# Diagonals of two heads as units under one mask product, four row slots, rows loaded by two engines, chunk-wise experts, and a tail among the maxima

## What is computed

```python
q, k, v = (x @ Wq.T + bq), (x @ Wk.T + bk), (x @ Wv.T + bv)      # 16 heads of depth 8
scores = einsum("bqhd,bkhd->bhqk", q, k) * attn_scale[0]
scores = where((qb >= kb) & (ik - iq - 2 * (kb - qb) >= 1), -inf, scores)   # chunks of 64
x = layernorm(x + (softmax(scores) @ v) @ Wo.T + bo)
s = sigmoid(x @ gate_weight.T)          # top 4 of 8 groups, then top 6 of 32, weights scaled by 2.5
routed = sum_e combine[:, e] * ((silu(x @ gate_e.T) * (x @ up_e.T)) @ down_e.T)
x = layernorm(x + routed + shared_expert(x))
```

## Time and profile before

| what | value |
|---|---|
| median of three runs | 492.0 us |
| profiled execution: its own time, and its span | 491.96 us, 490.0 us |
| first matmul of maxima | 32.6 us |
| first matmul of exponentials | 69.3 us |
| end of the last maxima | 262.4 us |
| end of the last values | 310.0 us |
| expert loop at its regular pace | from 321.4 us |
| PE, DVE, ACT, POOL busy | 422.9, 343.7, 220.7, 131.6 us |

### The profile page before, as it was taken

One profiled execution on the slowest core, in us unless ns is written; L12 is line 12 of the kernel. 1 busy time (PEld: TensorE's weight loads), 2 busy tenths in 40 slices (PEclk: granted clock), 3 DMA queues, 4 the chain that ended last, 5 costly groups with the idle time before them and its releaser, 6 DMA issues.

```text
span 490.0 us, 7996 instructions
## 1 busy us (share of the span) xinstructions
PE 422.9 (86%) x2856; PEld 218.9 (45%) x2856; DVE 343.7 (70%) x763; ACT 220.7 (45%) x299; POOL 131.6 (27%) x232
## 2 busy tenths in 40 slices
PE   6339979998698789798899997789999999999992
PEld 2225432433233233232333452467767666666661
DVE  3826978997588758589586448167768967865763
ACT  4600026675467647467477678322235233223220
POOL 4000014826545557444335434000000000000000
PEclk9855558999689979799799999899999999999998
DMA  4352430020211202101000000143213233443330
GB/s 142 131 183 96 113 96 3 4 93 7 62 51 34 84 7 71 50 3 61 7 1 3 1 1 3 44 137 88 106 70 107 102 119 105 135 134 101 110 108 21
DMA packets 27180, 34.26 MB, mean 70 GB/s; under 512 B 5893, under 2 KB 16261, under 8 KB 27141
## 3 DMA queue, kind: packets, MB, share of 16 engines
q1 hardware_dynamic: 26512, 33.41, 21.7%
q10 hardware_dynamic: 628, 0.34, 0.3%
HBM read 29.08 MB, written 4.46 MB: 68 GB/s over the span
## 4 chain that ended last, share of the span: by engine, by line
PE 60%; DMA 10%; DVE 9%; SPq 9%; POOL 4%; issue 4%; ACT 2%; POOLq 0%; DVEq 0%; ACTq 0%
PE ps L1235 12%; PE ps L1140 10%; PE ps L1100 8%; SPq L516 7%; PE ps L1207 6%; PE ps L1209 6%; PE ps L1208 6%; DVE mx L827 6%; DMA rows_k<-scratch 5%; PE ps L1123 4%; DMA w_raw<-in_unitT 2%; PE ps L1104 2%; PE ps L1160 2%; SPq L550 1%; ACT probs L727 1%
## 5 line engine op out<-in xcount | busy, mean ns | idle before, releaser
L827 DVE TENSOR_REDUCE mx<-ps 128x1 f32<-128x512 f32 (+3 forms) x320 | 180.9, 630 | 56.3 <-PE ps L1104 53.7
L727 ACT ACTIVATE probs<-ps 128x1024 f32<-128x1024 f32 (+2 forms) x160 | 143.5, 943 | 82.9 <-PE ps L1123 82.2
L1100 PE MATMUL ps<-rows_k,rows_q 48*128 48x512 bf16 (+3 forms) x384 | 111.9, 378 | 35.2 <-DMA rows_k<-scratch 26.7
L1140 PE MATMUL ps<-probs,Vg 128*32 128x512 f32 (+3 forms) x768 | 87.0, 526 | 7.5 <-POOL probs L625 6.5
L795 ACT ACTIVATE sg<-ps 128x512 f32<-128x512 f32 x68 | 40.8, 599 | 101.5 <-PE ps L1209 100.3
L1123 PE MATMUL ps<-rows_q,rows_k 51*128 51x512 bf16 (+3 forms) x384 | 72.9, 350 | 3.8 <-issue 2.5
L1207 PE MATMUL ps<-x1hi,w_hi 128*128 128x512 f32 x136 | 74.9, 551 | 0.0
L1100 PEld LDWEIGHTS ps<-rows_k,rows_q 48*128 48x128 bf16 x384 | 31.7, 99 | 95.5 <-DVE mx L827 55.3
L1035 DVE TENSOR_TENSOR au<-ps,sg 128x512 f32<-128x512 f32 x64 | 44.1, 689 | 38.0 <-PE ps L1235 37.0
L1235 PE MATMUL ps<-hh,w_down 128*128 128x512 f32 x136 | 69.8, 595 | 0.8 <-DVE hh L1040 0.8
L621 POOL TENSOR_SCALAR_AFFINE_SELECT probs<-probs 64x512 f32<-64x512 f32 x64 | 42.6, 666 | 69.0 <-ACT probs L727 66.6
(11 more groups left out here) (106 smaller groups left out, 316.7 us busy)
## 6 DMA issues: line engine op xcount, KB each, us to landing
comb_rows<-weights SPq DMA_DIRECT2D x128, 128.0 KB, 2.9
scratch<-oT SPq DMA_DIRECT2D x8, 384.0 KB, 3.0
w_raw<-in_unitT SPq DMA_DIRECT2D x17, 128.0 KB, 2.3
rows_q<-scratch SPq DMA_DIRECT2D x16, 96.0 KB
rows_k<-scratch SPq DMA_DIRECT2D x16, 96.0 KB
w_down<-in_unitT SPq DMA_DIRECT2D x1, 1088.0 KB, 7.7
xT<-in_xT SPq DMA_DIRECT2D x4, 256.0 KB, 3.9
rows_q<-scratch SPq DMA_DIRECT2D x16, 64.0 KB
```

Source lines behind the costliest of these rows:

```text
L727: act.activation(dst, src, ACT.Exp).then_inc(exps_ready, 1)
L827: dve.tensor_reduce(m_[:, part, j:j + per, qt], src, AX.X, ALU.max).then_inc(max_read, 1)
L1100: mm = pe.matmul(bank(b, m, at), rows_q[f:f + ROWS, s, p + qt * P:p + (qt + 1) * P], rows_k[f:f + ROWS, s, p + k0:p + k0 + m], start=True, ...
L1140: mm = pe.matmul(ps[STRIP * j:STRIP * (j + 1), VALUES * BANK:VALUES * BANK + m], Vg[:, g % 2, kt, j, :], probs[:, (NB * g + b) % SLOTS, j, ...
```

## The change

- **Units of the maxima.** A diagonal of 128 columns is a part of its own, always for two heads in one bank; the mask is added by one matmul of 256 columns (`identb` times `mask_qk`, broadcast over both heads), which opens the accumulation. The other keys follow in up to two more parts. NM becomes 48. `mx` gets three parts, and one `tensor_reduce` joins them.
- **Last group.** The last group's units are ordered with the first 512 queries ahead, and its maxima are joined, transposed, split and stored in two halves (`TOPS`); half of these stores is issued by ACT.
- **Row slots and loads.** NS is 4. Group 0's `rows_k` is issued by ACT, its `rows_q` by SP; waits for stored q and k parts are apart. Biases are loaded from ACT's queue. The x and constant loads and `w_down` come after the stores of group 0's maxima and the rows of group 3.
- **Front.** All eight projections have a bank of their own; all v projections come before the maxima. The last two splits (n = 6, 7) are POOL's.
- **Expert weights.** RAW = 4 `w_raw` buffers, and seven unit splits come ahead of POOL's first mask.
- **Tail.** The tail goes by chunk of four tiles. `CHUNK_STEPS` of chunk 0 stand one after each odd unit of the maxima from unit 7 of group 6 on, the steps of chunk 1 up to `logit` after the last top; the router of chunk 1 and all of chunks 2 and 3 are in the expert loop (`LOOP`). The router works on four tiles.
- **Order.** LEAD is gone; the planner's costs are changed.
- **Memory.** `sg`, `hh`, `au`, `moT` use the first two row slots; the router's work area is a tensor of its own.

```diff
-NS = 3
+NS = 4
+RAW = 4
-        for part, (k0, m) in enumerate([(P * qt, min(n, BANK)), (P * qt + BANK, n - BANK)]):
+        k0, n = P * qt, T - P * qt
+        for part, most in ((0, P), (1, BANK), (2, BANK)):
+            m = min(n, most)
+            if m:
+                units += [(js, qt, k0, m, part) for js in ([(0, 1), (2, 3)] if 2 * m <= BANK else [(0,), (2,), (1,), (3,)])]
+            k0, n = k0 + m, n - m
+MAXU = [max_units([*LOW, *HIGH] if g_ >= SPLIT_FROM else [*HIGH, *LOW]) for g_ in range(NG)]
+TOPS = [(g_, h_) for g_ in range(NG) for h_ in ((0, 1) if g_ >= SPLIT_FROM else (None,))]
+CHUNK_STEPS = ([("out", t) for t in range(QUAD)] + [("turn", 0), ("proj", 0), ("stat", 0), ("aggr", 0), ("norm", 0),
+                                                   ("x1T", 0), ("logit", 0)]
+               + [("route", t) for t in range(8)] + [("comb", 0)])
+            if tail and (g, n) >= TAIL_FROM and n % 2:
+                steps.append(tail.pop(0))
+TAIL_FROM = (NG - 2, 6)
+LOOP_BASE = {1: 0, 2: 3, 3: 18}
+FIRST_FILLS = 7
-        if k / len(MSEQ) * NG - i["e"] / NE > LEAD and i["e"] < len(ev):
-            return far
...
@@ sync
+            for n in range(NC):
+                sp.wait_ge(parts_ready, n + 1)
+                store_parts(n)
+            load_rows(0)
+            load_rows(1)
+            for n in range(NC, 6):
+                sp.wait_ge(parts_ready, n + 1)
+                store_parts(n)
+            for n in (6, 7):
+                sp.wait_ge(rest_ready, n - 5)
+                store_parts(n)
+            for u in range(RAW):
+                load_unit(u)
+            load_rows(2)
             for what, g, n in pool_order:
+                if what == "w" and n + RAW < NU:
+                    load_unit(n + RAW)
                 elif what == "split":
                     store_max(g)
                     if g == 0:
-                        sp.dma_start(w_down[:, :, :], a["unitT"][:, :, 2 * P:]).then_inc(down_loaded, 16)
+                        load_rows(3)
+                        load_consts()
...
@@ scalar
+            for n in range(5):
+                copy_projection(n)
+            copy_values(0)
+            copy_values(1)
+            copy_projection(5)
+            act.wait_ge(ones_set, NS)
+            act.wait_ge(k_stored[0], 32)
+            load_k(act, 0)
...
@@ tensor, max_step
-                        for c in range(2):
-                            mm = pe.matmul(bank(b, CHUNK, at + c * CHUNK), pick[f:f + CHUNK, c, :],
-                                           mask_k[f:f + CHUNK, :], start=False, stop=c == 1)
+                if part == 0:
+                    pe.matmul(dst.rearrange("p (j m) -> p j m", m=m), identb[:, :],
+                              mask_qk[:, :].unsqueeze(1).to_broadcast([P, len(js), P]), start=True, stop=False)
+                for at, j in enumerate(js):
+                    f, p = ROW_HALF * (j // PAIRS), j % PAIRS * T
+                    mm = pe.matmul(dst[:, at * m:(at + 1) * m], rows_q[f:f + ROWS, s, p + qt * P:p + (qt + 1) * P],
+                                   rows_k[f:f + ROWS, s, p + k0:p + k0 + m], start=part > 0,
+                                   stop=part > 0 or at == len(js) - 1)
```

More of the change, by code:

```diff
@@ new lines, with max_steps @@
+ON_BANK = ("unit", "top", "out", "turn", "proj", "x1T", "logit", "comb")
+ROUTED = CHUNK_STEPS.index(("route", 0))
+def max_steps():
+    steps = []
+    tail = [(kind, 0, i) for kind, i in CHUNK_STEPS]
+    for g in range(NG):
+        for n in range(NM):
+            steps.append(("unit", g, n))
+            if n == TOP_AFTER and g:
+                steps.append(("top", len(TOPS_BEFORE[g]) - 1, 0))
+            if g >= SPLIT_FROM and n == NLOW + TOP_AFTER:
+                steps.append(("top", len(TOPS_BEFORE[g]), 0))
+            if tail and (g, n) >= TAIL_FROM and n % 2:
+                steps.append(tail.pop(0))
+    steps.append(("top", len(TOPS) - 1, 0))
+    return steps + tail + [(kind, 1, i) for kind, i in CHUNK_STEPS[:ROUTED]]
@@ L118 @@
+LOOP.sort(key=lambda a: a[0])
+LOOP_BANKED = [step for _, step in LOOP if step[0] in ON_BANK]
+LOOP_BANKS = (4, 5)
 LAST = -3e38
-FILLS = [("x", t) for t in range(QUAD)] + [("w", u) for u in range(NU)]
+FIRST_FILLS = 7
+FILLS = ([("w", u) for u in range(NU - 5)] + [("x", t) for t in range(QUAD)] + [("w", u) for u in range(NU - 5, NU)])
 def attention_order():
     ev, vv = ([(g, n) for g in range(NG) for n in range(k)] for k in (NE, NB))
-    hop, rows_latency, load = 240, 3500, 6000
-    LEAD = 1.6
+    hop, rows_latency, load = 240, 6000, 6000
+    exp_slack, mask_slack = 300, 600
@@ L137, in attention_order @@
     fills = list(FILLS)
-    tt = [(0, n) for n in range(COMB)]
-    i = {"e": 0, "m": 0, "v": 0, "t": 0}
-    lag = {"out": 800, "turn": 900, "proj": 1100, "x1T": 1500, "logit": 700, "comb": 0}
-    streams = {"e": ev, "m": MSEQ, "v": vv, "t": tt}
+    for _ in range(FIRST_FILLS):
+        pool_order.append((fills[0][0], 0, fills.pop(0)[1]))
+        clock["pool"] += 1300
+    pool_order.append(("values", 0, 0))
+    clock["pool"] += 800
+    i = {"e": 0, "m": 0, "v": 0}
+    streams = {"e": ev, "m": MSEQ, "v": vv}
@@ L167, in run_sides @@
             elif what == "top":
-                top_read[g] = end + hop
-                todo["pool"].append(("split", g, 0, end + hop, 1500))
+                read["top", g, 0] = end + hop
+                todo["pool"].append(("split", g, 0, end + hop, 2500))
             elif what == "split":
                 split_done[g] = end + hop
+                if TOPS[g][1] is not None:
+                    todo["act"].append(("rows", g, 0, end + hop, 2000))
+            elif what == "root":
+                root_done[g] = end + hop
+            elif what in CHUNK_KINDS:
+                act_done[what, g] = end + hop
             elif what == "mask":
@@ L665, in bias_x @@
                 pool.wait_ge(x_biased, q + 1)
-            values(0)
+            for n in (6, 7):
+                split_rest(n)
             for what, g, n in pool_order:
@@ L1259, in _ @@
                     down(i - 2)
-                if i in TAIL_AT:
-                    tail_step(1, TAIL_AT[i])
+                for at, step in LOOP:
+                    if at == i and step[0] in ON_BANK:
+                        loop_step(step)
             back(NC - 1)
```

843 lines of the change are left out of this document (456 added, 387 removed).

## The result

The changed kernel takes 495.84 us (median of 15 executions, 492.82 to 500.29) against 490.99 us for the kernel before beside it (15 executions, 487.25 to 494.58). The ratio is 1.0108, with a 95% interval of 1.0079 to 1.0137: slower by 1.1%, where 453 us were forecast. A few executions are slow, over 1.5% above the fastest of their kernel (one of the 15 here, one of 10 in e1, two of 10 in e7, four of 10 in e11): medians and ranges take them in, ratios leave them out. The profiled execution took 494.91 us with a span of 493.1 us.

A forecast was written before the change was run, and what follows sets the result against it. Maxima on PE and DVE, row waits and the lowered clock bounded the front and middle, PE the experts. Last values at 277.9, plus 3.5 start, 161.4 loop, 8.5 end and 1.96 gave 453 us; range 436 to 482.

The forecast's parts named there:

- Router and tail among the maxima: First batch's router, moved among maxima: some 6 us of DVE time fits free time; costs up to 6 us otherwise.
- ACT's issues for the half tops: Last group's maxima: six DMA issues on ACT per half, 0.6 us each, inside ACT's slack.
- Period: One group of maxima: 25.0 us at full clock plus reductions and mask product, 26.0 us, over 6.6 groups.
- The mask product: Maxima on PE: 16 matmuls of 256 columns a group add 0.4 us, between -0.1 and +1.1.
- The eight small reductions: Maxima on DVE: 48 reductions instead of 40 add 0.6 us a group to the period, between 0 and 1.24.
- Rows: Front: issuing rows_k from ACT beside SP gains 3.5 us, between 0 (transfers bind) and 4.0 (issue binds).
- The seven early unit splits on POOL: Front: the splits lie in POOL's idle time before its first mask and cost nothing.
- Clock: Without row waits PE's clock stays at 1.00 from about 75 us; 2.5 us lost once at the first exponentials.
- the fourth slot: Groups of maxima: rows loaded a whole group ahead, so row waits vanish and a period is 25.0 us at full clock.
- SP's queue: Group 1's exponentials wait 3 us (0 to 12) behind queued loads; over 30 us after group 0's would disprove the forecast.
- The slower case: Rival, chance 0.06: maxima starve DVE, period passes 31.9 us; at 35.95 us the time is 519 us.
- Exponentials falling behind: Rival, chance 0.10: half a group more exponentials left after the maxima and 6 us of router, 16 us: 469 us.

The follow-up runs named there:

- e1: Changed kernel with chunk 0's tail and router steps moved behind the last group's top: 489.69 us, ratio 0.9955 to the kernel before.
- e7: Changed kernel with group 1's rows held until group 0's landed, first unit loads ahead of them, four early POOL splits instead of seven: 492.48 us, ratio 1.0028.
- e11: e8 with three row slots instead of four, group g+3 loaded behind group g's exponentials: 493.57 us, ratio 1.0023 to the kernel before.
- e2: Changed kernel with one whole top for the last group, stored by SP, instead of two halves: 486.75 us, ratio 0.9911.
- e15: e8 with chunk 0's steps behind every fifth unit of the last group instead of every third: 454.59 us, ratio 0.9275.
- e13: Changed kernel with two 64-column half-row mask matmuls per diagonal score instead of the full-row product for two heads: 487.23 us, ratio 0.9934.
- e9: e8 with one 128-column mask matmul over all rows behind each diagonal score instead of two half-row ones: 515.05 us, ratio 1.0504.
- e14: e8 with separate diagonal units (48 a group), half-row masks kept, and chunk 0's steps behind every fifth unit: 463.71 us, ratio 0.9476.
- e12: e8 with SP issuing group 0's rows_k behind its rows_q, ACT none: 455.39 us, ratio 0.9290.
- e8: Changed kernel with old units and masks, whole last top, chunk 0's steps among last group's maxima, e7's front, some loop steps one index later: 455.49 us, ratio 0.9285.

## Why the prediction was wrong

Between 453 and the 494.91 us of the profiled execution lie 41.9 us: first exponentials (71.6 instead of 62.9) 8.7, group 6's maxima (45.3 instead of 26.0) 19.3, the other 5.6 groups of maxima (27.9 instead of 26.0) 10.4, from the last maxima to the last values 3.0, start of the experts 2.8 instead of 3.5, loop 162.2 instead of 161.4, end 8.9 instead of 8.5.

- **Router and tail among the maxima, "costs nothing new".** This is the step that failed first. I priced the router's DVE time at 6 us and counted on what DVE has free. In group 6 DVE is busy 10.8 us beyond its reductions, router and the tail's other steps together, where group 5 left it 5.4 us idle; and PE, which I did not price there, had 0.5 us idle in 27.4. So most of the delay is work that did not fit (11.5 of 15.9 us on DVE), the rest waits. What makes it dear is the order: in one stream of maxima and tail steps the steps hold the group's top, and everything of that group. The bound of 6 us was too low by a factor of three: 19.3 us beyond the forecast, of which e1 gave back 7.5 because the next two causes stood behind it.
- **ACT's issues for the half tops, "inside its slack".** ACT has no slack in the stage in which it sets the pace, which the sum itself said a paragraph earlier (19.28 us a group). Twelve issues of 0.76 us and the unit order that goes with them: 9.7 us (e2). My price for one issue was 0.6 us and near; the place was wrong.
- **Period.** The base was right: 24.3 to 24.8 us a group at full clock in e15, against 25.0 forecast. The mask product was put at 0.4 us (-0.1 to 1.1) and is 1.3 to 1.9 (e13): one of 256 columns takes 0.283 us by its row, and the next matmul starts 0.22 us after it, not the 0.11 I derived from an overlapping pair. The Trainium skill's rule, "TensorE: Matmul & The Clock Gate", Part 3, "The mechanism", was the better guide here: e9 and e13 agree with it, above the upper end I gave it. The eight small reductions were put at 0.6 (0 to 1.24) and cost 0.5 to 1.6 in groups 3 to 5 (e14 against e15).
- **Rows.** "3.5 us nearer to the issue" was the wrong end: the second queue gives nothing (e12), and group 1's rows, which I named as competing and did not price, take 3 us away (e7). The Trainium skill, "DMA: Bandwidth & Descriptors", "Issuing engines are not separate DMA queues", says that issuing from several engines saves only issue time; e12 agrees. The seven early unit splits on POOL, put at nothing, hold group 0's split until 63.80 us, though its copy on ACT ended at 62.45. The biases won nothing either: `bk` lands at 7.12 us on ACT's queue, later than the 6.77 of the earlier trace rows.
- **Clock.** "Without a wait the clock has no reason to fall" agrees with the middle of the run (1.00 in groups 3 to 5), and in the holes there were waits that the forecast did not have. But e2 and e9, in the rows at the end, contradict it as a rule: the clock fell, and stayed low, with PE busy throughout by the trace.
- **Right:** the fourth slot. Undoing it on e8 costs 36 us (e11), and in the changed kernel groups run without row waits from group 1 on. The v projections left the first maxima: from the first reduction to the join group 0 takes 25.1 us instead of 26.0 in spite of the slower mask. SP's queue did no harm: group 1's exponentials start 29.6 us after group 0's, under the 30 I set. Start of the experts and loop came within 1 us, although of the loop's 0.8 us too much e8 gave 1.3 back.
- **The rivals.** The slower case had its chance of 0.06 for DVE starved past 31.9 us a group; DVE's idle time, 0.06 to 0.11 us a reduction in groups 3 to 5, was no cause. Exponentials falling behind was the nearest in kind, but priced at half a group and 6 us. Each was a term of the sum going wrong by itself; that two terms priced at nothing lay on the path of the same engine's order was not among them.

The sum's value was within reach: with the three edits taken back or moved (mask and units, split, place of the tail), the front mended and steps of the loop one index later, the other parts of the change give 454.6 to 455.5 us.

## What to carry to other kernels

When work is moved among other work of engines whose order is fixed, price it twice. First its busy time, on every engine that it uses, against what that engine has free in that very stretch. Then the order: ask which later step cannot pass it, and who starves behind that one. An issue of a DMA on a computing engine is computing time of that engine (here 0.76 us of ACT for each), and has to be checked against the stage in which that engine sets the pace. And a matmul that spans all rows of the array, put among matmuls that overlap in halves, has to be costed by the time from its start to the next one's, read from such a matmul and not from a pair that overlaps.

## What was not expected of the hardware

- The lower clock can last under a PE that is always busy. In e9 PE was busy 39.92 of the 40 us from 80 to 120 us at a granted clock of 0.50 (1.2 GHz), and in e2 the clock fell in the middle of a busy stretch, though PE had been busy 5.00 of 5.00 us before it:

```profile
225.00:230.00 5.00, 5.00 (x52) 2.62 (x45) 2.99 (x9) 4.16 (x7) 1.25 (x3) 1.00 0.02 3
230.00:235.00 5.00, 5.00 (x29) 0.99 (x32) 4.02 (x12) 2.70 (x5) 2.27 (x4) 0.54 0.00 0
```

  What decided it there, no run shows.
- Two half-row masks of 64 columns cost less than one full-row mask of 128: replacing 64 of the one kind by 32 of the other lengthened a group by 4.4 us. Columns alone do not explain it: the next matmul starts 0.22 us after a product of 256 columns and, in e9 at full clock, 0.16 us after one of 128, while in the expert loop one of 512 columns follows another after 0.23 us. Why, no run shows.
- DMAs whose issue ends 1.5 us earlier, on a queue of their own, landed no earlier (e8 against e12).
